# K and V block diagonals with the block index outermost, V stored head by head with its ones column

## The reference, cut to what matters

```python
H, D = (32, 16)                                   # heads, head width
q = (x @ Wq.T + bq).reshape(B, S, H, D)           # B = 4, S = 512
k = (x @ Wk.T + bk).reshape(B, S, H, D)
v = (x @ Wv.T + bv).reshape(B, S, H, D)
scores = jnp.einsum('bshd,bsgd->bshg', q, k) * inv_sqrt_d
scores = jnp.where(scores > THRESH, scores, -jnp.inf)
attn = jax.nn.softmax(scores, axis=-1)
out = jnp.einsum('bshg,bsgd->bshd', attn, v).reshape(B, S, Hd)
```

## Time and profile before

| | |
|---|---|
| time, median of 3 runs | 2551.21 us (2549.51 to 2552.23) |
| the profiled execution: time, span | 2552.01 us, 2550.4 us |
| busy share: PE, PEld, DVE, ACT, POOL | 80%, 66%, 62%, 40%, 43% |
| stage qkv, first half, from the barrier's end to the next stage | 1023.4 to 1097.4 us |
| stage heads, first half | 1097.4 to 1192.0 us |
| stage heads, second half | 2340.9 to 2433.2 us |

### The profile page before, as it was taken

How to read it: one execution, slowest core, us unless ns; L and a number is a source line. 1 busy time by engine, 2 the same in 40 slices (tenths; PEclk the granted TensorE clock), 3 DMA queues, 4 the chain that set the end, 5 groups by cost and what they waited for, 6 DMA issues and landing times. The chain is left out here.

```text
span 2550.4 us, 34479 instructions
## 1 busy us (share of the span) xinstructions
PE 2029.6 (80%) x11904; PEld 1680.7 (66%) x11904; DVE 1572.9 (62%) x3747; ACT 1029.2 (40%) x2380; POOL 1108.5 (43%) x866
## 2 busy tenths in 40 slices
PE   7489999999999942954447999999999996357634
PEld 1378888888888832743335888888888885346434
DVE  1666666666666669244645666666666666852645
ACT  1255555555555522122114555555555553131211
POOL 0454555555554534132325555555554544341322
PEclk9699999999999976965768999999999999678566
DMA  5300100010001001285031100010001001024921
GB/s 228 108 17 26 42 18 26 18 41 26 17 26 42 17 30 54 79 91 125 15 119 34 33 17 26 21 39 25 17 26 42 17 26 38 23 72 90 94 87 42
DMA packets 188903, 123.30 MB, mean 48 GB/s; under 512 B 107172, under 2 KB 151204, under 8 KB 187700
## 3 DMA queue, kind: packets, MB, share of 16 engines
q1 hardware_dynamic: 174356, 101.26, 16.1%
q10 hardware_dynamic: 14368, 19.78, 2.4%
HBM read 100.01 MB, written 21.01 MB: 47 GB/s over the span
## 5 line engine op out<-in xcount | busy, mean ns | idle before, releaser
L965 POOL TENSOR_TENSOR gqa_rot<-gqa_rot,consts 128x512 f32<-128x512 f32 x160 | 209.1, 1307 | 640.8 <-ACT gqa_rot L786 640.7
L802 ACT ACTIVATE gqa_prob<-gqa_prob,gqa_nmax 128x128 f32<-128x128 f32 (+3 forms) x512 | 282.0, 552 | 198.6 <-DVE gqa_nmax L887 198.6
L887 DVE CUSTOM_DVE_ANT_0 gqa_prob<-gqa_pS,consts 128x128 f32<-128x128 f32 (+3 forms) x512 | 220.2, 486 | 73.6 <-PE gqa_pS L686 72.6
L430 PE MATMUL ln_pT<-consts,ln_xn 128*128 128x128 f32 x256 | 59.8, 422 | 253.9 <-DVE ln_xn L409 253.9
L895 DVE TENSOR_TENSOR gqa_ptl<-gqa_pT,gqa_pth 128x384 fp32r<-128x384 f32 (+1 forms) x384 | 218.3, 597 | 31.7 <-ACT gqa_pth L812 27.1
L430 PEld LDWEIGHTS ln_pT<-consts,ln_xn 128*128 128x128 f32 x256 | 51.3, 225 | 262.3 <-DVE ln_xn L409 262.3
L812 ACT CAST gqa_pth<-gqa_pT 128x384 fp32r<-128x384 f32 (+1 forms) x384 | 182.7, 511 | 94.4 <-PE gqa_pT L701 94.3
L968 POOL TENSOR_TENSOR gqa_full<-gqa_full,gqa_rot 128x512 f32<-128x512 f32 x160 | 206.7, 1292 | 12.6
L740 PE MATMUL gqa_pW<-woh,gqa_oh 128*128 128x512 f32 x504 | 202.7, 402 | 9.0 <-DVE first_y L912 9.0
L659 PE MATMUL gqa_pj<-first_hh,wqh 128*128 128x512 f32 x496 | 205.5, 414 | 0.0
L740 PE MATMUL gqa_pW<-woh,gqa_ol 128*128 128x512 f32 x504 | 197.3, 392 | 0.0
(11 more groups left out here) (221 smaller groups left out, 5299.9 us busy)
## 6 DMA issues: line engine op xcount, KB each, us to landing
raw_q<-in_wq SPq DMA_DIRECT2D x16, 1024.0 KB, 5.3
raw_o<-in_wo SPq DMA_DIRECT2D x16, 1024.0 KB, 5.1
mod_wm<-in_wmod SPq DMA_DIRECT2D x8, 1536.0 KB, 19.9
raw_kv<-in_wkv SPq DMA_DIRECT2D x16, 512.0 KB, 6.5
x<-in_x SPq DMA_DIRECT2D x4, 1024.0 KB, 6.4
kp<-qkv_rest SPq DMA_DIRECT2D x16, 256.0 KB, 2.3
qp<-qkv_rest SPq DMA_DIRECT2D x16, 256.0 KB, 2.3
vp<-qkv_rest SPq DMA_DIRECT2D x16, 256.0 KB, 2.3
```

The costliest lines, as they stand in the source:

```text
L802: ins = nc.scalar.activation(p, p, ACT.Exp, scale=-1.0, bias=nmax[r][:, i:i + 1], accum_out=den[r][:, i:i + 1])
L887: nc.vector.tensor_tensor_reduce(prob[r][:, P_OFF[i]:P_OFF[i] + w], pS[s][:, c:c + w], held.mask[:, T - w:T], -1.0, LARGEST, ALU.add, ALU.min,
L965: nc.gpsimd.tensor_tensor(rot[r % 2][:], rot[r % 2][:], held.sinT, ALU.mult).then_inc(sined, 1)
```

## The change

`kd` and `bd` get the block index as their outermost index behind the partition, so that what one load writes into a partition is one contiguous piece: 4096 bytes of `kd` (32 pieces of 128 bytes before) and 2176 bytes of `bd` (32 pieces of 64 bytes before). For `bd` the DRAM tensor `vp` is laid out head by head, with the ones column in it (17 numbers instead of 16), so the source of a load is contiguous too. The separate ones column memsets in stage heads go. The matmuls now read their moving operand with a step between the four blocks.

In return stage qkv must write V in that layout: DVE writes 16 of every 17 numbers of `rest`, whose ones are set once at the stage's start, and SP stores each V item with four transfers, in pieces of 17 numbers (68 bytes), where one transfer of contiguous rows of 2048 bytes did it before. The order of the matrices becomes V, K, Q.

```diff
-QKV_ORDER = (1, 0, 2)
+QKV_ORDER = (2, 1, 0)
...
-        rest = [st.sb(f"rest{i}", [P, T]) for i in range(NB)]
+        rest = [st.sb(f"rest{i}", [P, H1 * VW]) for i in range(NB)]
...
                     if w == 2:
-                        dst = a["vp"][b].rearrange("(t r) x -> r t x", r=KT)[m]
-                        sp.dma_start(dst, src[:]).then_inc(stored[n % NB], 16)
+                        for r in range(4):
+                            sp.dma_start(a["vp"][b, r, :, :, m].rearrange("g l x -> l g x"),
+                                         values(n)[r * LO:(r + 1) * LO]).then_inc(stored[n % NB], 16)
...
                     if n >= 8:
-                        if n - 8 < FIRST_V:
-                            pe.wait_ge(left, n - 7)
+                        if n - 8 < NV:
+                            pe.wait_ge(turned, n - 7)
                         else:
-                            pe.wait_ge(turned, n - 7)
+                            pe.wait_ge(left, n - 7 - NV)
...
+                for i in range(NB):
+                    nc.vector.memset(values(i)[:, :, D1:], 1.0).then_inc(ones, 1)
+                dve.wait_ge(ones, NB)
                 for n in range(N):
                     if n >= NB:
-                        dve.wait_ge(stored[n % NB], 16 * (n // NB))
-                    if n < FIRST_V:
-                        dve.wait_ge(left, n + 1)
-                        nc.vector.transpose(rest[n % NB][:], flat[n % NB][:]).then_inc(turned, 1)
+                        dve.wait_ge(stored[n % NB], stored_by[n - NB])
+                    if n < NV:
+                        dve.wait_ge(full, n + 1)
+                        nc.vector.tensor_tensor(values(n)[:, :, 0:D1], ps[n % 8][:].rearrange("p (g x) -> p g x", g=H1),
+                                                vbias[:].rearrange("p (g x) -> p g x", g=H1), ALU.add).then_inc(turned, 1)
...
-        kd = [st.sb(f"kd{i}", [P, 4 * LU, 4, H1]) for i in range(NU)]
-        bd = [st.sb(f"bd{i}", [P, 4 * LU, 4, VW]) for i in range(NU)]
+        kd = [st.sb(f"kd{i}", [P, 4, 4 * LU, H1]) for i in range(NU)]
+        bd = [st.sb(f"bd{i}", [P, 4, 4 * LU, VW]) for i in range(NU)]
...
-                eng.dma_start(kd[u % NU][D1 * j:D1 * j + D1, :, j], a["kp"][b, j, :, ls, :].rearrange("d l (r h) -> d (l r) h", h=H1)
+                eng.dma_start(kd[u % NU][D1 * j:D1 * j + D1, j], a["kp"][b, j, :, ls, :].rearrange("d l (r h) -> d (l r) h", h=H1)
...
-                eng.dma_start(bd[u % NU][32 * r:32 * r + 32, :, r, 0:D1], src).then_inc(v_in[u], 16)
+                src = a["vp"][b, r, :, l0:l0 + LU].rearrange("g l j x -> g (l j) x")
+                eng.dma_start(bd[u % NU][32 * r:32 * r + 32, r], src).then_inc(v_in[u], 16)
...
-                                           kd[u % NU][0:ROWS, 4 * (l0 + l) + r].rearrange("p j g -> p (j g)"), start=True, stop=True)
+                                           kd[u % NU][0:ROWS, :, 4 * (l0 + l) + r, :], start=True, stop=True)
...
-                                           bd[u % NU][:, s0 + 4 * l + j].rearrange("p r x -> p (r x)"), start=True, stop=True)
+                                           bd[u % NU][:, :, s0 + 4 * l + j, :], start=True, stop=True)
```

More of the change, by code:

```diff
@@ L1051 @@
 LO = 32
+VW = D1 + 1
 def stage_qkv(nc, held, a, ws):
@@ L1062, in stage_qkv @@
         flat = [st.sb(f"flat{i}", [P, T]) for i in range(NB)]
-        rest = [st.sb(f"rest{i}", [P, T]) for i in range(NB)]
+        rest = [st.sb(f"rest{i}", [P, H1 * VW]) for i in range(NB)]
         ps = [st.ps(f"ps{i}", [P, T]) for i in range(8)]
-        w_lo, b_scaled, full, left, turned = (st.sem(n) for n in ("w_lo", "b_scaled", "full", "left", "turned"))
+        w_lo, b_scaled, ones, full, left, turned = (st.sem(n) for n in ("w_lo", "b_scaled", "ones", "full", "left", "turned"))
         stored = [st.sem(f"stored{i}") for i in range(NB)]
@@ L1068, in stage_qkv, with values @@
         N = len(items)
-        FIRST_V = 2 * HB * KT
+        NV = HB * KT
+        total, stored_by = [0] * NB, []
+        for n, (w, b, m) in enumerate(items):
+            total[n % NB] += 64 if w == 2 else 16
+            stored_by.append(total[n % NB])
+        def values(n):
+            return rest[n % NB][:].rearrange("p (g x) -> p g x", g=H1)
         with nc.Block() as block:
@@ L1112, in _ @@
                 act.wait_ge(b_scaled, 1)
-                for n, (w, b, m) in enumerate(items[:FIRST_V]):
+                for n in range(NV, N):
+                    w, b, m = items[n]
                     act.wait_ge(full, n + 1)
-                    if n >= NB:
+                    if n >= NV + NB:
                         act.wait_ge(turned, n - NB + 1)
@@ L1147 @@
 CHUNKS = UNITS1 * CU
-VW = D1 + 1
 def stage_head_attention(nc, held, a):
@@ L1175, in stage_head_attention @@
         k_zeroed, v_zeroed = [st.sem(f"k_zeroed{i}") for i in range(NU)], [st.sem(f"v_zeroed{i}") for i in range(NU)]
-        ones = [st.sem(f"ones{i}") for i in range(NU)]
         s_full, copied, top_done, shifted, exp_done, masked, turned = (st.sem(n) for n in (
@@ L1194, in load_values @@
             if u < NU:
-                eng.wait_ge(ones[u], 4)
+                eng.wait_ge(v_zeroed[u], 1)
             for r in range(4):
-                t0 = (LO * r + l0) * KT
-                src = a["vp"][b, t0:t0 + KT * LU, :].rearrange("t (g x) -> g t x", g=H1)
-                eng.dma_start(bd[u % NU][32 * r:32 * r + 32, :, r, 0:D1], src).then_inc(v_in[u], 16)
+                src = a["vp"][b, r, :, l0:l0 + LU].rearrange("g l j x -> g (l j) x")
+                eng.dma_start(bd[u % NU][32 * r:32 * r + 32, r], src).then_inc(v_in[u], 16)
         with nc.Block() as block:
@@ L1247, in weigh @@
                         for j in range(4):
-                            mm = pe.matmul(pO[c % NO][32 * j:32 * j + 32, l].rearrange("p r x -> p (r x)"), pt[c % NR][:, 4 * l + j, :],
-                                           bd[u % NU][:, s0 + 4 * l + j].rearrange("p r x -> p (r x)"), start=True, stop=True)
+                            mm = pe.matmul(pO[c % NO][32 * j:32 * j + 32, l], pt[c % NR][:, 4 * l + j, :],
+                                           bd[u % NU][:, :, s0 + 4 * l + j, :], start=True, stop=True)
                     mm.then_inc(o_full, 1)
@@ L1265, in _ @@
                 zeros = held.mask[:, 0:P].rearrange("p (o x) -> p o x", o=1).to_broadcast([P, 4 * LU, P])
-                nc.scalar.copy(kd[2][:].rearrange("p s j g -> p s (j g)"), zeros).then_inc(k_zeroed[2], 1)
+                nc.scalar.copy(kd[2][:].rearrange("p j (s r) g -> p (j s) (r g)", r=4), zeros).then_inc(k_zeroed[2], 1)
                 for c in range(CHUNKS + 1):
@@ L1309, in _ @@
                 nc.vector.memset(bd[0][:], 0.0).then_inc(v_zeroed[0], 1)
-                dve.wait_ge(v_zeroed[0], 1)
-                for r in range(4):
-                    nc.vector.memset(bd[0][32 * r:32 * r + 32, :, r, D1:], 1.0).then_inc(ones[0], 1)
                 for c in range(CHUNKS + 6):
@@ L1326, in _ @@
                     nc.gpsimd.memset(bd[i][:], 0.0).then_inc(v_zeroed[i], 1)
[L1327 to L1330, removed]
                 for c in range(CHUNKS):
@@ L1585 @@
     a["row_scale"] = nc.dram_tensor("row_scale", (D,), F32).ap()
-    for n, shape in (("qp", (HB, 4, D1, LO, P)), ("kp", (HB, 4, D1, LO, P)), ("vp", (HB, T, D))):
+    for n, shape in (("qp", (HB, 4, D1, LO, P)), ("kp", (HB, 4, D1, LO, P)), ("vp", (HB, 4, H1, LO, 4, VW))):
         a[n] = nc.dram_tensor(n, shape, F32).ap()
```

11 lines of the change are left out of this document (5 added, 6 removed).

## The result

| | before | after |
|---|---|---|
| time, median | 2551.21 us | 2560.84 us |
| lowest to highest of 7 runs | 2548.96 to 2553.84 | 2558.20 to 2564.15 |
| ratio to before, 95% interval | | 1.0038 (1.0026 to 1.0049) |
| span of the profiled execution | 2550.4 us | 2558.6 us |

2512 was forecast, from 2503 to 2546. Both stages moved, and in opposite directions. A stage is measured here from DVE's first instruction in stage qkv, or SP's first load in stage heads, to the first load of the stage behind.

The account below looks back on a forecast made before the run. Stage heads was taken as bound by many small load pieces, stage qkv by PE. Gains on loads and the `o` stall, less 0.7 us per half, made 38.6 us off 2552.0; after adjusting to the median, 2512, range 2503 to 2546.

Parts of the forecast that it names:

- The loads: Stage heads: with large contiguous pieces, PE's waits for kd go except the first, saving 19.7 and 17.7 us.
- The stall for `o`: Stage heads: DVE's wait for the store of `o` before dividing chunk 8 shrinks from 6.3 to 5.0 us, 1.3 per half.
- the next in line: Stage heads: once loads fit, PE itself is the limit at 2.93 us per chunk, DVE close behind at 2.61.
- The stepped operand of the matmuls: Stage heads: matmuls reading runs with a step between them cost nothing; at a tenth more, 4 us per half.
- The cover of the V stores: Stage qkv: V stores of up to 6.5 us per item are hidden; longer ones lengthen each half.
- The formula: Stage qkv: the eighth V item has landed at 1031 + 8s, s being the V store's time per item in us.
- The term that was mis-sized: Stage qkv: a V item's store of 4096 pieces takes 5.2 us, at 793 packets per us, so it costs nothing.
- The sum: Whole kernel: 19.7 + 17.7 + 2 x 1.3 - 2 x 0.7 = 38.6 us less than 2552.0, giving 2513.4.
- rival 4: Stage qkv: V stores from 8.9 us per item on make the kernel slower, 2584 us at 10.9; chance 0.12.
- Rival 2: Stage heads: PE's clock rises from 0.50 and DVE sets the pace, up to 3 us per half, 2506; chance 0.08.
- Rival 5: Stage heads: loads are bound by bytes, a unit takes 7.5 us, only some 7 us are left, 2543; chance 0.05.

Follow-up runs that it names:

- the single store: Changed kernel with the V scratch laid out so that one transfer of 128 partitions stores an item, instead of four of 32: 2545.78 us, ratio 0.9984.
- 64 at 68: Changed kernel with V stored in 64 byte pieces at 68 byte steps, ones set in bd, 64 byte loads: 2555.88 us.
- the 96 byte kernel: Changed kernel with V pieces and steps of 96 bytes (24 numbers), padding written and loaded: 2517.24 us, ratio 0.9868 to the kernel before.
- The K half alone: Kernel before with only kd's new layout, V stored and loaded as before, order K, Q, V: 2529.07 us, ratio 0.9921.

## Why the prediction was wrong, by its own steps

- **The loads** (19.7 and 17.7 us): right. With the 1.3 for `o`, 21.0 and 19.0 were forecast and 19.9 and 17.4 measured. Two short waits before units 1 and 2 stayed, 2.4 us in all, more than the "few tenths" that were allowed; the first scores came 8.0 us after the stage's start instead of 9.9, 0.6 better than said.
- **The stall for `o`**: 4.8 us (5.0 expected, 6.3 before). PE at 2.93 us per chunk, the next in line, as said. The stepped operand of the matmuls costs nothing: scores 1.86 us and weighing 1.07, as in the earlier trace rows.
- **The cover of the V stores**: right. The formula puts the eighth V item at 1031 + 8s; with the 9.4 us of the packet rate and this execution's stage, which began 1.9 us earlier, that is 1104.3 against 1103.86 measured. 8 x (9.3 - 6.5) + 0.7 is 23.1 us per half, and 23.3 and 22.5 were measured. With the 8.5 us of the single store and the 8.1 of 64 at 68 the formula says 16.7 and 13.5 more than before, and 16.7 and 13.8 were measured. (The prediction's own terms give a cover of (1094.9 - 1042) / 8 = 6.6 us rather than 6.5, which is 0.9 us per half.) All layouts that took under 6.5 us were hidden.
- **The term that was mis-sized: "I take 5.2 us: the piece size is nearest, and the rate is one that was held for 46 us."** It measured 9.3. The rate of loads of 64 and 128 byte pieces, whose edges in DRAM all lie on multiples of 64 bytes, was carried over to 68 byte writes, of which one in eight starts on a multiple of 32. The run with half of the V stores shows that their time is the loss, and nine other layouts show that it goes by where the pieces lie in DRAM: at the same count and size, steps of 128 bytes bring 36.6 ns down to 21.9, and pieces whose edges are multiples of 32 cost about 14. The sum was right but for this term: with it gone, the 96 byte kernel's profiled execution took 2515.3 us against the 2513.4 of the sum.
- **The rivals.** What happened is rival 4, "the same place, from s = 8.9 on", to which 0.12 was given; it came in just behind its edge, not at the 10.9 us of the store of `o`. Rival 2 did not come: the granted clock stayed 0.50 through 35 us of PE work without a gap (1136.55 to 1171.7). Rival 5 did not: a unit's 784 KB fit its 5.86 us, and with pieces of 128 bytes 1024 KB fit it nearly as well in one half (76.2 us, against 82.0 in the other). Its price was set too low: before, the waits make a unit 5.86 + 18.5 / 7 = 8.5 us and not 8, so at 7.5 us about 14 of the 37.4 us would have been left and not 7.

PE's clock in stage heads after (1119 to 1194 us), columns as above:

```profile
1119.00:1194.00 75.00, 47.01 (x1024) 36.36 (x1024) 48.55 (x82) 21.64 (x33) 29.14 (x19) 0.50 0.55 116
```

## What to carry to other kernels

When a layout is changed so that loads become contiguous, the small pieces move to the store; ask how many there are, how long each takes, and what covers them, and look at where each piece starts and ends, not only at its size. In this kernel a row of 17 numbers was a trap: padded to 24, so that every edge is on a multiple of 32 bytes, it moves 41% more bytes, and 2.6 times as many pieces are stored per us. When a kind of transfer has no price in the trace and the bounds enclose the break-even (here 2.7 to 10.9 us around 6.5 and 8.9), the middle is a guess: measure that term first, or change only the part that doesn't need it. The K half alone gave 0.8% without a new store.

## What was unexpected of the hardware

- A store in small pieces costs by where the pieces' edges lie in DRAM: 14.2 and 14.1 ns per piece and engine for 96 and 128 bytes with edges on multiples of 32, 11.6 or less for 64 bytes; 20.8 to 23.0 with a ragged end or edges on 16; 34.7 to 36.6 in steps of 68 bytes. The Trainium skill, DMA: Bandwidth & Descriptors, section Specifications, puts a read-modify-write below 512 bytes; here 96 byte pieces went out at 107 GB/s and 68 byte ones at 29, so that size alone does not tell them apart. The Trainium skill, same page, section How a descriptor splits into AXI transactions, counts in beats of 32 bytes (its rules there are for reads), which fits the fastest class. Which part of the chip spends the time was not measured.
- The source side did not matter in the same way: the 64 byte pieces were read at steps of 68 bytes on chip, and were as fast as any (11.6 ns).
- 35 us of PE work without a gap left the granted clock at 0.50, the 1.2 GHz level.
